# Moving the pieces of the next batch between the attention units of a fused audio tower

## The chip, the core and the metric

The kernel runs on one core of a Trainium2 chip. The time is the device time of one launch in microseconds (us); lower is better. TensorE is called PE, VectorE DVE, ScalarE ACT, GpSimd POOL; SP is the queue of SyncE, which here only issues DMAs.

## What is computed

The input is 8 rows of 120,000 samples, each cut into 1500 frames of 80. All arithmetic is float32 in the reference:

```python
h = layernorm(x_frames @ W.T + b) * gamma + beta          # 8 x 1500 x 256
h = gelu(h)                                               # exact, with erf
z = _layernorm(h)
Q, K, V = z @ Wq.T + bq, z @ Wk.T + bk, z @ Wv.T + bv      # 16 heads of 16
attn = softmax(Q K^T / 4)                                 # 1500 x 1500 per head
h = h + (attn V) @ Wo.T + bo
h = h + _L0_ffn_ref(_layernorm(h), ...)
```

The last line is computed in both kernels as `h + layernorm(_layernorm(h)) * ln_g + ln_b`: the routed attention inside `_L0_ffn_ref`, whose weights are drawn with a spread of 0.02, is in neither, and its weights are no inputs of them.

## The kernel before

**Units and rounds.** The attention of a batch is cut into 12 units (the text counts them from 0 to 11): 4 groups of 4 heads by 3 chunks of 500 queries. Unit u has group u // 3 and chunk u % 3, so units 9, 10 and 11 are the last group of a batch. A unit has 8 rounds (0 to 7). In each round PE multiplies six pairs of key tile and head into six PSUM banks (`scores`, L810, matmuls of float16), ACT takes the exponential of two banks at a time (lines 473, 476 and 481, in this order, are the three of a round), and PE multiplies the result with the values (`attend`, L834, float32): one tile of keys in an even round (4 matmuls side by side on the 128 columns of the array), two in an odd one. PE runs up to four scores matmuls ahead, those of the first two exponentials of the next round.

**Other work in between.** Everything else is cut into pieces, and the table `PLAN` says behind which round of which unit each is done. The pieces of batch b+1 are spread over the units of batch b, and so are the outputs of the batch before: 6 `tok` (tokenizer matmul of two tiles of frames, L755, then its layer norm on DVE with POOL's root between, L503 to L518), 6 `turn` (transposes, L764, and a copy on DVE, L542), 12 `qk` (projection in two halves, L771, each in a round of its own; behind the second half DVE writes it as two float16 tensors, L551 and L553, and SP stores them to a scratch in HBM), 12 `val` (values, L780 and L558), 3 `norm` and one `flag` (a bound on the scores' size, L787 and L793, that selects the softmax without a maximum), 12 `out` (output projection, L800, and the last layer norm, L612 to L625). Behind every fourth `qk`, POOL squares all four (L367).

**One bank for the pieces.** All pieces of a unit use one PSUM bank, 7 - n % 2 for unit n of the whole run. The other bank of the two collects the unit's attention. So PE waits in `beside` before each piece until DVE has freed the bank of the piece before, and before the first piece of a unit until DVE has taken the sums of the unit before out of that bank (`take_sums`, L595 and L596). DVE takes the pieces in the same order as PE issues them, and does between them: `invert` (four reciprocals, L603, behind rounds 1 to 4, and with the fourth the product L606), and three times in a batch, where the table `NORMS` says so, the layer norm of four tiles of the next batch (`norm_stats` and `norm_apply`, L526 to L535, with POOL's root between). These three stand behind the pieces and the reciprocal of their round.

**GELU.** ACT does the GELU of a whole batch at one place (`GELU`), between two loads of its table.

**SP's queue.** It is in program order too: the stores of `qk`; behind round 4 of a unit `store_attended`, which waits until DVE has finished L606 of the unit before; and `load_group`, which loads Q and K of the next four heads. The last scores that PE issues in round 7 of unit 2, 5, 8 and 11 are those of the next group and wait for that load (`s_ld`). For the groups 1 to 3 it is issued at the start of unit 1, 4 and 7. For the first group of the next batch:

```python
if u == NU - 1 and b + 1 < B:
    load_group((b + 1) * NG)
```

Of the kernel before, what the change touches and what calls it, by code (L numbers as in the profile page):

```python
# [5 lines left out]
def audio_tower(nc, x, tok_wT, tok_b, tok_g, tok_be, wqT, bq, wkT, bk, wvT, bv, woT, bo, ln_g, ln_b, out):  # L6
# [47 lines left out]
    place(2, 4, "turn", 0)
    place(2, 6, "turn", 1)
    place_qk(0, 3, 0, 2)
    place_qk(1, 3, 3, 4)
# [6 lines left out]
    place(5, 2, "val", 3)
    place(5, 3, "turn", 2)
    place(5, 4, "turn", 3)
    place(5, 6, "val", 4)
    place_qk(4, 6, 0, 2)
    place_qk(5, 6, 3, 4)
    place(6, 6, "val", 5)  # L70
    place_qk(6, 7, 0, 2)
    place_qk(7, 7, 3, 4)
    place(7, 6, "val", 6)
    place(8, 0, "val", 7)
    place(8, 1, "norm", 1)
    place(8, 2, "turn", 4)
    place(8, 3, "turn", 5)
    place_qk(8, 8, 4, 6)
    place_qk(9, 9, 0, 2)
    place_qk(10, 9, 3, 4)  # L80
    place(9, 6, "val", 8)
    place_qk(11, 10, 0, 2)
    place(10, 3, "val", 9)
    place(10, 4, "val", 10)
    place(10, 6, "val", 11)
    place(11, 1, "norm", 2)
    place(11, 5, "flag", 0)
# [50 lines left out]
    with ExitStack() as ctx:  # L138
# [86 lines left out]
        def at(sem_, count):  # L225
            return count + TOTAL.get(sem_, 0) if second[0] else count
# [6 lines left out]
        def _(sp):  # L233
# [38 lines left out]
            def store_out(b, c):  # L272
                k = b * NC + c
                sp.wait_ge(s_y, at(s_y, CT * (k + 1)))
                sp.dma_start(out_v[b, :, c * CT:(c + 1) * CT, :], Y[:, k % 2, :, :]).then_inc(s_yst[k % 2], 16)

            def run():
                load_x(1)
                for i in range(4 * NC):
                    store_halves(0, i)  # L280
                load_group(0)
                for n in range(B * NU):
                    b, u = n // NU, n % NU
# [211 lines left out]
        def _(dve):  # L495
# [11 lines left out]

            def tok_norm(b, i, bank):
                p, e = i % 2, hslot(b, 2 * i)
                dve.wait_ge(s_r1, at(s_r1, b * (NT // 2) + i + 1))  # L510
                for j in range(2):
                    ins = dve.scalar_tensor_tensor(out=Hs[:, e + j, :], in0=PS[0:T, bank, j * D:(j + 1) * D],  # L512
                                                   scalar=mv1[:, p, j, 0:1], in1=g_tok[:, :],
                                                   op0=ALU.subtract, op1=ALU.mult)
                ins.then_inc(s_free, 1)
                dve.drain()
                for j in range(2):
                    ins = dve.scalar_tensor_tensor(out=Hs[:, e + j, :], in0=Hs[:, e + j, :],  # L518
                                                   scalar=rs1[:, p, j:j + 1], in1=be_tok[:, :],
                                                   op0=ALU.mult, op1=ALU.add)  # L520
                ins.then_inc(s_h1, 1)
# [463 lines left out]
```

## Time and profile before

| | |
|---|---|
| median of 3 runs | 2575.2 us (2572.72 to 2577.77) |
| the profiled execution | 2566.03 us |
| its span, first to last instruction | 2564.3 us |
| PE busy | 2270.0 us, 89% |
| ACT busy | 2154.9 us, 84% |
| DVE busy | 1222.3 us, 48% |
| mean granted clock of TensorE | 0.952 of full |

Busy time of PE is that of pipelined matmuls whose ends are modelled, so 89% doesn't mean that it computed for 89% of the time. ACT's 2304 exponentials are the longest chain of one engine. A unit is measured here from the start of its first L473 to that of the next unit.

### The profile page before, as it was taken

To read this page: it belongs to the slowest core of one execution; us is meant where nothing else is said; L and a number is where in the kernel's file an instruction comes from. 1 tells how busy PE (TensorE), PEld (TensorE's weight loads), DVE (VectorE), ACT (ScalarE), POOL (GpSimd) and SP (SyncE) were. 2 spreads that over 40 slices of the span, in tenths; PEclk is the share of its full clock that TensorE was granted. 3 is DMA by queue.
4 is the path that set the end of the run, shared out by engine and by line. 5 is a ranking of instruction groups with operands and counts; after the bars stand their busy time and mean duration, and the time that the engine had idled before them with its cause. 6 is when DMAs were issued, how large, how long until landed. Compare 5 with 4: busy or idle time off the path is not lost.

```text
span 2564.3 us, 48095 instructions
## 1 busy us (share of the span) xinstructions
PE 2270.0 (89%) x19500; PEld 680.2 (27%) x19500; DVE 1222.3 (48%) x2362; ACT 2154.9 (84%) x2332; POOL 374.1 (15%) x495
## 2 busy tenths in 40 slices
PE   4589998999989998899988999899998999898892
PEld 1222222222322222222222222222222222222221
DVE  6444435544465444643456444654446444452224
ACT  0099997999969998899978999699997999799991
POOL 2211002211121111210122110211112111120002
PEclk7799999999989999999989999899998999999997
DMA  2402211222122122122112221212212212111101
GB/s 60 128 17 63 63 37 39 53 63 63 38 69 56 42 59 53 46 77 53 41 45 53 63 63 39 58 40 56 67 33 70 54 51 53 52 47 31 31 5 30
DMA packets 89956, 132.09 MB, mean 52 GB/s; under 512 B 12295, under 2 KB 69702, under 8 KB 89726
## 3 DMA queue, kind: packets, MB, share of 16 engines
q1 hardware_dynamic: 87190, 127.11, 19.1%
q8 instruction: 156, 2.56, 0.4%
q10 hardware_dynamic: 2536, 1.83, 0.3%
q14 instruction: 74, 0.61, 0.1%
HBM read 55.16 MB, written 61.44 MB: 45 GB/s over the span
## 4 chain that ended last, share of the span: by engine, by line
PE 40%; issue 34%; ACT 9%; POOL 9%; DVE 4%; POOLq 1%; DMA 1%; SPq 1%; DVEq 0%; ACTq 0%
PE PS L834 19%; PE PS L810 12%; PE PS L771 5%; ACT prob L476 4%; ACT prob L473 3%; POOL sq L367 3%; POOL Y L375 2%; PE PS L780 2%; POOL rs L377 2%; DVE HL L553 1%; POOL rs L348 1%; DVE HL L551 1%; POOLq L376 1%; DMA qk_halves_scratch<-HL 1%; ACT prob L481 1%
## 5 line engine op out<-in xcount | busy, mean ns | idle before, releaser
L834 PE MATMUL PS<-prob,Vst 125*32 125x500 f32 x9216 | 1149.8, 602 | 1.9 <-ACT prob L476 1.1
L481 ACT ACTIVATE prob<-PS 125x1000 f32<-125x1000 f32 x768 | 775.0, 1009 | 208.9 <-PE PS L810 208.3
L810 PE MATMUL PS<-QA,KA 64*125 64x500 f16 x4608 | 783.1, 413 | 105.2 <-DMA KA<-qk_halves_scratch 46.0
L473 ACT ACTIVATE prob<-PS 125x1000 f32<-125x1000 f32 x768 | 773.6, 1007 | 108.3 <-PE PS L810 108.2
L476 ACT ACTIVATE prob<-PS 125x1000 f32<-125x1000 f32 x768 | 782.8, 1019 | 0.0
L810 PEld LDWEIGHTS PS<-QA,KA 64*125 64x125 f16 x4608 | 258.7, 133 | 896.1 <-ACT prob L473 419.2
L603 DVE RECIPROCAL On<-Den 128x125 f32<-128x125 f32 x384 | 344.5, 918 | 10.2 <-issue 2.7
L834 PEld LDWEIGHTS PS<-prob,Vst 125*32 125x32 f32 x9216 | 221.9, 109 | 441.4 <-issue 272.9
L551 DVE TENSOR_SCALAR HL<-PS,b_qk 128x500 f16<-128x500 f32 x96 | 70.9, 738 | 397.9 <-PE PS L771 333.8
L367 POOL TENSOR_TENSOR sq<-HL 128x2000 bf16<-128x2000 f16 x24 | 84.5, 3522 | 1184.8 <-DVE HL L553 1184.8
L771 PE MATMUL PS<-zT,w_qk 128*32 128x500 f32 x1536 | 196.4, 593 | 1.2 <-DVE zT L542 1.2
L595 DVE LOAD_MASK_SELECT Den<-PS x96 | 1.3, 13 | 312.3 <-PE PS L834 312.3
L800 PE MATMUL PS<-w_o,oT 128*32 128x256 f32 (+1 forms) x1536 | 103.5, 391 | 37.6 <-DMA oT<-On 23.1
L780 PE MATMUL PS<-w_v,zT 128*32 128x256 f32 (+1 forms) x1536 | 104.7, 396 | 25.8 <-DVE Osb L596 25.8
L372 POOL TENSOR_SCALAR rs<-mv 125x1 f32<-125x1 f32 x96 | 26.7, 278 | 602.8 <-DVE mv L616 602.8
L558 DVE TENSOR_TENSOR Vst<-PS,b_v 125x256 f32<-125x256 f32 x96 | 40.2, 422 | 147.7 <-PE PS L780 147.7
L606 DVE TENSOR_TENSOR On<-On,Osb 128x500 f32<-128x500 f32 x96 | 101.0, 1052 | 7.9 <-issue 0.9
L755 PE MATMUL PS<-w_tok,X 81*32 81x256 f32 (+1 forms) x768 | 60.3, 445 | 31.7 <-DVE Hs L512 18.3
L625 DVE SCALAR_TENSOR_TENSOR Y<-Hs,rs,Y 125x256 f32<-125x256 f32 x96 | 79.7, 830 | 7.5 <-issue 0.4
L612 DVE TENSOR_TENSOR Hs<-Hs,PS 125x256 f32<-125x256 f32 x96 | 38.4, 400 | 93.8 <-PE PS L800 93.5
L771 PEld LDWEIGHTS PS<-zT,w_qk 128*32 128x32 f32 x1536 | 49.9, 112 | 115.9 <-issue 87.9
L542 DVE COPY zT<-PS 128x500 f32<-128x500 f32 x48 | 32.6, 679 | 94.4 <-PE PS L764 94.4
(78 smaller groups left out, 1068.4 us busy)
## 6 DMA issues: line engine op xcount, KB each, us to landing
qk_halves_scratch<-HL SPq DMA_DIRECT2D x384, 125.0 KB
QA<-qk_halves_scratch SPq DMA_DIRECT2D x64, 375.0 KB, 5.0
KA<-qk_halves_scratch SPq DMA_DIRECT2D x64, 375.0 KB, 7.2
oT<-On SPq DMA_DIRECT2D x384, 31.2 KB, 2.0
out<-Y SPq DMA_DIRECT2D x24, 500.0 KB
X<-in_x SPq DMA_DIRECT2D x8, 468.8 KB, 8.1
w_qk<-in_wqT ACTq DMA_DIRECT2D x2, 128.0 KB, 3.8
w_qk<-in_wkT ACTq DMA_DIRECT2D x2, 128.0 KB, 3.9
```

The source lines that it names most:

```text
L367: pool.tensor_tensor(sq[:, :, :], HL[:, :, 0, :], HL[:, :, 0, :], ALU.mult).then_inc(s_sq, 1)
L473: act.activation(prob[0:T, 6 * p:6 * p + 2, :], PS[0:T, 0:2, 0:QC], ACT.Exp, scale=scl)\
L476: act.activation(prob[0:T, 6 * p + 2:6 * p + 4, :], PS[0:T, 2:4, 0:QC], ACT.Exp, scale=scl)\
L481: act.activation(prob[0:T, 6 * p + 4:6 * p + 6, :], PS[0:T, 4:6, 0:QC], ACT.Exp, scale=scl)\
L551: dve.tensor_scalar(HL[:, i % 4, 0, :], PS[:, bank, 0:QC], bias, None, ALU.add)
L603: dve.reciprocal(On[:, part * T:(part + 1) * T], Den[:, part * T:(part + 1) * T])
L606: dve.tensor_tensor(On[:, :], On[:, :], Osb[:, :], ALU.mult).then_inc(s_on, 1)
L771: ins = pe.matmul(PS[lo:hi, bank, 0:QC], w_qk[:, c, w, m * 128 + lo:m * 128 + hi], zT[:, c, :], start=(c == 0), stop=(c == KC - 1))
L780: last = pe.matmul(PS[lo:hi, bank, 0:D], zT[:, c, t + lo:t + hi], w_v[:, c, :], start=(c == 0), stop=(c == KC - 1))
L800: last = pe.matmul(PS[lo:hi, bank, 0:D], oT[:, m, e * T + lo:e * T + hi], w_o[:, m, :], start=(m == 0), stop=(m == KC - 1))
L810: last = pe.matmul(PS[0:T, bank, 0:QC], KA[rows, G % 2, h // 2, t * T:(t + 1) * T], QA[rows, G % 2, h // 2, c * QC:(c + 1) * QC], start=Tr ...
L834: last = pe.matmul(PS[lo:lo + 2 * HD, 6 + n % 2, 0:QC], Vst[:, b % 2, t, g * HG + j, :], prob[0:T, (HG * t + j) % 12, :], start=(t == 0), ...
```

## The change

It moves pieces to other rounds, moves two of the three layer norms on DVE earlier and one later against the rounds, moves the GELU from round 7 of unit 1 to round 2 of unit 2, issues the load of the next batch's first group at the end of unit 10 in place of unit 11, stores the last outputs of a batch in unit 3 in place of unit 2, and in `tok_norm` on DVE puts the wait for POOL's root behind the first of two passes (a drain stands where it was).

```diff
-    for j, r in enumerate((0, 2, 3, 4)):
+    for j, r in enumerate((0, 2, 4, 6)):
         place(11, r, "out", j)
         place(0, r, "out", 4 + j)
-    for j in range(2):
-        place(11, 5 + j, "tok", j)
-        place(0, 5 + j, "tok", 2 + j)
-        place(1, 2 * j, "tok", 4 + j)
-    place(1, 4, "out", 8)
+    place(10, 4, "tok", 0)
+    place(11, 3, "tok", 1)
+    place(0, 3, "tok", 2)
     for j in range(3):
-        place(1, 6, "out", 9 + j)
+        place(1, 2 * j, "tok", 3 + j)
+        place(2, 1, "out", 9 + j)
+    place(1, 6, "out", 8)
...
-    NORMS = {(2, 0): 0, (4, 6): 1, (7, 6): 2}
-    GELU = (1, 7)
+    NORMS = {(2, 3): 0, (4, 4): 1, (6, 6): 2}
+    GELU = (2, 2)
...
-                    if u < 3 and b > 0:
-                        store_out(b - 1, u)
+                    if u in (0, 1, 3) and b > 0:
+                        store_out(b - 1, min(u, 2))
...
-                    if u == NU - 1 and b + 1 < B:
+                    if u == NU - 2 and b + 1 < B:
                         load_group((b + 1) * NG)
...
             def tok_norm(b, i, bank):
                 p, e = i % 2, hslot(b, 2 * i)
-                dve.wait_ge(s_r1, at(s_r1, b * (NT // 2) + i + 1))
+                dve.drain()
                 for j in range(2):
                     ins = dve.scalar_tensor_tensor(out=Hs[:, e + j, :], in0=PS[0:T, bank, j * D:(j + 1) * D],
                                                    scalar=mv1[:, p, j, 0:1], in1=g_tok[:, :],
                                                    op0=ALU.subtract, op1=ALU.mult)
                 ins.then_inc(s_free, 1)
                 dve.drain()
+                dve.wait_ge(s_r1, at(s_r1, b * (NT // 2) + i + 1))
```

The whole table, as pieces by unit and round (`/` parts rounds; qk3a and qk3b are the two halves of the fourth projection; N0, N1, N2 are DVE's layer norms):

| unit | before | after |
|---|---|---|
| 0 | 0 out, 2 out, 3 out, 4 out, 5 tok, 6 tok | 0 out, 2 out, 3 tok, 4 out, 6 out |
| 1 | 0 tok, 2 tok, 4 out, 6 three out, GELU ahead of 7 | 0 tok, 2 tok, 4 tok, 6 out |
| 2 | 0 N0, 4 turn, 6 turn | 1 three out, GELU ahead of 2, 3 N0, 6 turn |
| 3 | 0 qk0a, 2 qk0b, 3 qk1a, 4 qk1b, 6 val | 0 turn, 2 qk0a, 3 qk0b, 4 qk1a, 5 qk1b, 6 val |
| 4 | 0 qk2a, 2 qk2b, 3 qk3a, 4 qk3b, 6 val and N1 | 0 qk2a, 2 qk2b, 3 qk3a, 4 qk3b and N1, 5 val, 6 val |
| 5 | 0 val, 1 norm, 2 val, 3 turn, 4 turn, 6 val | 0 val, 1 norm, 2 turn, 3 turn, 4 qk4a, 6 qk4b |
| 6 | 0 qk4a, 2 qk4b, 3 qk5a, 4 qk5b, 6 val | 0 qk5a, 2 qk5b, 3 qk6a, 4 qk6b, 5 val, 6 val and N2 |
| 7 | 0 qk6a, 2 qk6b, 3 qk7a, 4 qk7b, 6 val and N2 | 0 qk7a, 2 qk7b, 3 val, 4 val, 6 turn |
| 8 | 0 val, 1 norm, 2 turn, 3 turn, 4 qk8a, 6 qk8b | 0 turn, 1 norm, 2 qk8a, 3 qk8b, 4 qk9a, 5 qk9b, 6 val |
| 9 | 0 qk9a, 2 qk9b, 3 qk10a, 4 qk10b, 6 val | 0 qk10a, 2 qk10b, 3 qk11a, 4 qk11b, 6 val |
| 10 | 0 qk11a, 2 qk11b, 3 val, 4 val, 6 val | 0 val, 1 norm, 2 val, 4 tok, 6 flag |
| 11 | 0 out, 1 norm, 2 out, 3 out, 4 out, 5 tok and flag, 6 tok | 0 out, 2 out, 3 tok, 4 out, 6 out |

Two places of it as the engines' own programs have them. The first is SP's queue at the end of the first batch, from the stores of the last projections on; oT<-On is the store of a unit's attention, QA and KA are the loads of a group. Before:

```order
148 L245 DMA qk_halves_scratch<-HL 8x16x500 [waits s_free]
149 L245 DMA qk_halves_scratch<-HL 8x16x500 x3
150 L269 DMA oT<-On 16x500 [waits s_on]
151 L269 DMA oT<-On 16x500 x3
152 L269 DMA oT<-On 16x500 [waits s_on]
153 L269 DMA oT<-On 16x500 x3
154 L258 DMA QA<-qk_halves_scratch 64x2x1500 [waits s_st,s_sc,s_ld]
155 L258 DMA QA<-qk_halves_scratch 64x2x1500
156 L258 DMA KA<-qk_halves_scratch 64x2x1500 x2
```

And in the change:

```order
148 L269 DMA oT<-On 16x500 [waits s_on]
149 L269 DMA oT<-On 16x500 x3
150 L269 DMA oT<-On 16x500 [waits s_on]
151 L269 DMA oT<-On 16x500 x3
152 L258 DMA QA<-qk_halves_scratch 64x2x1500 [waits s_st,s_sc,s_ld]
153 L258 DMA QA<-qk_halves_scratch 64x2x1500
154 L258 DMA KA<-qk_halves_scratch 64x2x1500 x2
155 L269 DMA oT<-On 16x500 [waits s_on]
156 L269 DMA oT<-On 16x500 x3
```

The load now stands ahead of the store of unit 10's attention (row 155) and behind that of unit 9's (row 150); before, it stood behind unit 10's (row 152).

The second place is DVE's queue in unit 4 of the first batch, from the second half of qk3 on; L526 to L535 are the layer norm N1, L595 and L596 take the sums of the unit, L558 takes a `val`. Before:

```order
192 L551 TENSOR_SCALAR HL<-PS,b_qk 128x500 [waits s_full,s_st]
193 L553 SCALAR_TENSOR_TENSOR HL<-PS,b_qk,HL 128x500
194 L603 RECIPROCAL On<-Den 128x125
195 L606 TENSOR_TENSOR On<-On,Osb 128x500
196 L558 TENSOR_TENSOR Vst<-PS,b_v 125x16x16 [waits s_full]
197 L526 BN_STATS st<-Hs 125x6 [waits s_ge]
198 L526 BN_STATS st<-Hs 125x6 x3
199 L529 BN_AGGR mv<-st 125x2 x4
200 L535 TENSOR_SCALAR z<-Hs,mv,rs 125x256 [waits s_r2]
201 L535 TENSOR_SCALAR z<-Hs,mv,rs 125x256 x3
202 L595 STREAM_SHUFFLE Den<-PS 128x500 [waits s_pv,s_on]
203 L596 COPY Osb<-PS 128x500
```

And in the change, where the lines of DVE from here on have a number that is higher by one:

```order
193 L552 TENSOR_SCALAR HL<-PS,b_qk 128x500 [waits s_full,s_st]
194 L554 SCALAR_TENSOR_TENSOR HL<-PS,b_qk,HL 128x500
195 L604 RECIPROCAL On<-Den 128x125
196 L607 TENSOR_TENSOR On<-On,Osb 128x500
197 L527 BN_STATS st<-Hs 125x6 [waits s_ge]
198 L527 BN_STATS st<-Hs 125x6 x3
199 L530 BN_AGGR mv<-st 125x2 x4
200 L536 TENSOR_SCALAR z<-Hs,mv,rs 125x256 [waits s_r2]
201 L536 TENSOR_SCALAR z<-Hs,mv,rs 125x256 x3
202 L559 TENSOR_TENSOR Vst<-PS,b_v 125x16x16 [waits s_full] x2
203 L596 STREAM_SHUFFLE Den<-PS 128x500 [waits s_pv,s_on]
204 L597 COPY Osb<-PS 128x500
```

The layer norm now stands ahead of the two takings of values (row 202); before, one of them stood ahead of it (row 196) and the next behind L596, in unit 5.

## Rows read from the trace of the kernel before

**Rows 1.** The page: busy time by engine, and two of its groups.

```profile
PE 2270.0 (89%) x19500; PEld 680.2 (27%) x19500; DVE 1222.3 (48%) x2362; ACT 2154.9 (84%) x2332; POOL 374.1 (15%) x495
...
L810 PE MATMUL PS<-QA,KA 64*125 64x500 f16 x4608 | 783.1, 413 | 105.2 <-DMA KA<-qk_halves_scratch 46.0
...
L558 DVE TENSOR_TENSOR Vst<-PS,b_v 125x256 f32<-125x256 f32 x96 | 40.2, 422 | 147.7 <-PE PS L780 147.7
```

**Rows 2.** Busy time by stretch: unit 3 of batch 7; all of batch 7; batch 2.

```profile
core 0: us, PE busy (x) PEld busy (x) DVE busy (x) ACT busy (x) POOL busy (x), PEclk, DMA share, GB/s
2311.25:2333.18 21.93, 19.48 (x148) 5.16 (x144) 5.29 (x8) 21.93 (x26) 0.00 (x0) 1.00 0.34 77
2238.81:2509.60 270.79, 243.53 (x1926) 67.22 (x1924) 90.93 (x156) 263.33 (x288) 19.22 (x36) 1.00 0.12 28
723.90:1027.49 303.59, 282.49 (x2439) 84.45 (x2437) 151.94 (x293) 269.48 (x291) 46.24 (x60) 0.96 0.21 53
```

**Rows 3.** The same: batch 3, units 0, 1, 3, 5, 8, 11.

```profile
1027.49:1056.96 29.47, 26.52 (x250) 8.32 (x248) 17.74 (x38) 22.16 (x25) 7.30 (x14) 0.91 0.09 27
1056.96:1086.10 29.14, 24.45 (x244) 7.67 (x240) 19.94 (x48) 27.34 (x30) 7.97 (x16) 1.00 0.27 65
1108.02:1130.85 22.83, 22.74 (x196) 6.41 (x192) 8.77 (x13) 21.99 (x25) 0.00 (x0) 1.00 0.17 50
1153.62:1179.84 26.22, 23.95 (x208) 7.60 (x204) 10.99 (x24) 22.05 (x26) 3.64 (x3) 0.93 0.05 10
1225.38:1251.54 26.16, 23.90 (x192) 7.15 (x188) 11.18 (x24) 22.02 (x25) 3.61 (x3) 0.93 0.05 10
1297.25:1331.12 33.87, 25.88 (x245) 8.59 (x237) 21.43 (x53) 22.17 (x25) 8.12 (x16) 0.88 0.24 56
```

**Rows 4.** Timeline, end of batch 3, SP and PE.

```profile
1318.55 2.40 SPq L269 DMA_DIRECT2D oT<-On  x4
1322.40 1.25 SPq L258 DMA_DIRECT2D KA<-qk_halves_scratch  x2
...
1321.67 0.37 PE L793 MATMUL PS<-ident,nm 128*1 128x128 f32 x1 [4.57 <-DVE Hs L512]
1330.41 1.09 PE L810 MATMUL PS<-QA,KA 64*125 64x500 f16 x4 [3.31 <-DMA KA<-qk_halves_scratch]
```

**Rows 5.** Timeline of PE in unit 4 of batch 3, rounds 4 and 5.

```profile
1144.06 0.85 PE L810 MATMUL PS<-QA,KA 64*125 64x500 f16 x6
1144.84 1.04 PE L834 MATMUL PS<-prob,Vst 125*32 125x500 f32 x8
...
1147.73 1.88 PE L834 MATMUL PS<-prob,Vst 125*32 125x500 f32 x16
```

**Rows 6.** Timeline, from there to unit 5: DVE, POOL and PE.

```profile
1148.49 3.52 POOL L367 TENSOR_TENSOR sq<-HL 128x2000 bf16<-128x2000 f16 x1 [51.34 <-DVE HL L553]
1149.33 3.21 DVE L606 TENSOR_TENSOR On<-On,Osb 128x500 f32<-128x500 f32 x1
1151.28 1.05 PE L780 MATMUL PS<-w_v,zT 128*32 128x256 f32 x16
1152.81 1.39 DVE L526 BATCH_NORM_STATS2 st<-Hs 125x6 f32<-125x256 f32 x4
1156.20 1.38 DVE L535 TENSOR_SCALAR z<-Hs,mv,rs 125x256 f32<-125x256 f32 x4 [1.55 <-POOL rs L354]
1158.83 1.73 PE L780 MATMUL PS<-w_v,zT 128*32 128x256 f32 x16 [1.86 <-DVE Osb L596]
```

**Rows 7.** Unit 5 of batch 1, by stretch as in rows 2.

```profile
547.84:572.48 24.64, 22.43 (x208) 7.26 (x204) 11.00 (x24) 22.06 (x26) 3.65 (x3) 1.00 0.05 12
```

**Rows 8.** Timeline of DVE in the prologue: the second and the third `tok`.

```profile
22.16 0.87 DVE L512 SCALAR_TENSOR_TENSOR Hs<-PS,mv,g_tok 125x256 f32<-125x256 f32 x2 [1.21 <-POOL rs L348]
23.12 0.88 DVE L518 SCALAR_TENSOR_TENSOR Hs<-Hs,rs,be_tok 125x256 f32<-125x256 f32 x2
...
26.20 0.88 DVE L512 SCALAR_TENSOR_TENSOR Hs<-PS,mv,g_tok 125x256 f32<-125x256 f32 x2 [1.20 <-POOL rs L348]
```

More of the change, by code:

```diff
@@ L42, in place_qk @@
         place(u, r1, "qk", i, True)
-    for j, r in enumerate((0, 2, 3, 4)):
+    for j, r in enumerate((0, 2, 4, 6)):
         place(11, r, "out", j)
         place(0, r, "out", 4 + j)
-    for j in range(2):
-        place(11, 5 + j, "tok", j)
-        place(0, 5 + j, "tok", 2 + j)
-        place(1, 2 * j, "tok", 4 + j)
-    place(1, 4, "out", 8)
-    for j in range(3):
-        place(1, 6, "out", 9 + j)
[L54 to L57, printed above, removed]
+    place(10, 4, "tok", 0)
+    place(11, 3, "tok", 1)
+    place(0, 3, "tok", 2)
+    for j in range(3):
+        place(1, 2 * j, "tok", 3 + j)
+        place(2, 1, "out", 9 + j)
+    place(1, 6, "out", 8)
+    place(2, 6, "turn", 0)
+    place(3, 0, "turn", 1)
+    place_qk(0, 3, 2, 3)
+    place_qk(1, 3, 4, 5)
     place(3, 6, "val", 0)
@@ L60, in audio_tower @@
     place_qk(3, 4, 3, 4)
-    place(4, 6, "val", 1)
-    place(5, 0, "val", 2)
+    place(4, 5, "val", 1)
+    place(4, 6, "val", 2)
+    place(5, 0, "val", 3)
     place(5, 1, "norm", 0)
[L64 to L69, printed above, removed]
-    place(6, 6, "val", 5)
[L71 to L74, printed above, removed]
-    place(8, 1, "norm", 1)
[L76 to L87, printed above, removed]
-    NORMS = {(2, 0): 0, (4, 6): 1, (7, 6): 2}
-    GELU = (1, 7)
+    place(5, 2, "turn", 2)
+    place(5, 3, "turn", 3)
+    place_qk(4, 5, 4, 6)
+    place_qk(5, 6, 0, 2)
+    place_qk(6, 6, 3, 4)
+    place(6, 5, "val", 4)
+    place(6, 6, "val", 5)
+    place_qk(7, 7, 0, 2)
+    place(7, 3, "val", 6)
+    place(7, 4, "val", 7)
+    place(7, 6, "turn", 4)
+    place(8, 0, "turn", 5)
+    place(8, 1, "norm", 1)
+    place_qk(8, 8, 2, 3)
+    place_qk(9, 8, 4, 5)
+    place(8, 6, "val", 8)
+    place_qk(10, 9, 0, 2)
+    place_qk(11, 9, 3, 4)
+    place(9, 6, "val", 9)
+    place(10, 0, "val", 10)
+    place(10, 1, "norm", 2)
+    place(10, 2, "val", 11)
+    place(10, 6, "flag", 0)
+    NORMS = {(2, 3): 0, (4, 4): 1, (6, 6): 2}
+    GELU = (2, 2)
     def batch_of(what, b, u):
@@ L94, in batch_of @@
         if what == "tok":
-            return b + 2 if u == NU - 1 else b + 1
+            return b + 2 if u >= NU - 2 else b + 1
         return b + 1
```

## The prediction, made before the changed kernel ran

> **What bounds the kernel now.** I read first the busy times of the page [rows 1]: ACT is busy 84%, PE 89%, DVE under half, so no engine is full, and the question is how far each unit is from what ACT alone needs. The busy times by stretch, cut at the starts of the units, tell that (in these rows stand the us, the busy us of each engine with its instructions, and the clock that was granted, 1.00 being 2.4 GHz). The floor is a unit of batch 7 with no piece in it: 21.93 us, and ACT is busy in all of it [rows 2]. A batch of twelve such units is 263 us. Batch 2 took 303.59, batch 7, which prepares no other batch, 270.79 [rows 2]. So each of the first seven batches loses some 40 us to the pieces, and the change can only win or lose among these.
>
> Where they are lost [rows 3]: a unit with pieces and nothing unusual takes 22.83 (units 3, 4, 6, 7, 9, 10 are all alike). Unit 0 takes 29.47, unit 1 29.14, units 5 and 8 26.2, unit 11 33.87. In unit 1 ACT is busy for 27.34 us, 5.4 more than elsewhere: that is the GELU, and it costs the same wherever it stands. The others are waits.
>
> Unit 11 and unit 0 are read in the timeline [rows 4]. PE waits 4.57 us ahead of the flag, since the `tok` before it holds the bank until DVE has POOL's root. Then it waits 3.31 us for the first group of the next batch: SP issued that load at 1322.40, behind the store that began at 1318.55 and had waited for DVE's L606, and it landed at 1330.4. Over all boundaries these waits are 46.0 us [rows 1]. Since the load lands 33 us after unit 11 began (1297.25), it ends the unit whatever the flag does. The granted clock of these two stretches is 0.88 and 0.91 of full [rows 3]: behind the waits TensorE runs for a while at 1.2 in place of 2.4 GHz.
>
> Units 5 and 8 [rows 6]: DVE begins the layer norm of round 6 of unit 4 at 1152.81 and ends its z at 1157.58, then takes the sums, and PE waits 1.86 us for those. If the clock stays at full the unit takes 24.64 [rows 7], at a granted 0.93 26.22 [rows 3].
>
> Why a normal unit costs 0.9 over the floor [rows 5, 6]: PE needs 0.85 for the six scores, 0.9 (a row of 1.04 that overlaps its neighbours) or 1.88 for the values, and 1.0 for a piece. Two rounds with one piece behind the even one are 5.5 us, ACT's two rounds also 5.5 (21.93 / 4). A second piece in the pair, behind the odd round, has no room: it costs 0.9 to 1.0. With two such pairs in one unit I count 1.8.
>
> **The change, part by part**, per batch, from the table of pieces.
>
> *Load in unit 10, flag in unit 10.* The load is issued behind the store of unit 9's attention. If DVE gives that free as late in unit 10 as it does in unit 11 now, 21.3 us in (1318.55 less 1297.25), and the issue and landing take the same 11.9 us as now, it lands 33 us after unit 10's start, 11 us into unit 11, and it is wanted in the last round, some 20 us in. All projections are stored by then. The flag has its `tok` two rounds behind it and doesn't wait. Unit 11 keeps one odd piece (0.9) and 0.3 for the round behind the `tok` (the bank comes free after 4.04 less 1.21 and 0.88, the period, wait and L518 of [rows 8], so 2.0; PE comes back after 0.85 and 0.9): 23.1 in place of 33.9, a gain of 10.8. Unit 0 loses its low clock, and one of two `tok` in neighbouring rounds: it keeps the odd piece (0.9), 0.3 behind the `tok`, and a wait at its start, since the last `out` now stands in round 6 of unit 11, and DVE finishes its layer norm before it takes the sums. That wait is between 0 and the 1.86 that a later DVE costs in [rows 6]; a layer norm of one tile is shorter than that of four, so I take 0.8. 23.9 in place of 29.5: a gain of 5.6.
>
> *Units 1 and 2.* GELU moves with its cover: the three `out` still run on PE while ACT is away. The first wait of unit 1 stays (now behind an `out`). I count nothing.
>
> *Unit 3* has pieces in rounds 3 and 5: +0.9. *Unit 6* too: +0.9. *Unit 8*: the same, but without the layer norm's wait: 26.2 to 23.9, a gain of 2.3. *Unit 10*: its pieces are light, a gain of 0.4.
>
> *Layer norm N1 in round 4 of unit 4* is what speaks against the change. DVE's queue holds it now ahead of the two takings of `val`. The round is the same in which POOL squares for 3.52 us and L606, normally 0.68, takes 3.21 until 1152.54 [rows 6]. The layer norm starts there as before (4.8 us from 1152.81 to 1157.58, no longer behind a `val` of 0.42 [rows 1]), z is done at 1157.2, the first `val` taken at 1157.6. PE wants the bank for the second `val` at 1151.28 [rows 6] plus the 1.0 of the new piece in round 5, at 1152.3. So it stands still for 5.3 us, and is 6.3 us later than before. ACT has two exponentials in hand, as always there, and loses all of it. A low clock comes on top: between 0 and 3 us; units 5 [rows 3, 7] show 1.6 behind a wait of 1.86, and behind a longer one I take 2. Unit 4: 22.8 to 31.1, a loss of 8.3. Unit 5 no longer has the wait: from 25.4 (the mean of the two above) to 22.8, a gain of 2.6.
>
> *N2 in round 6 of unit 6.* It does to unit 7 what N1 did to unit 5: a loss of 2.6 in place of those counted as gone in unit 8.
>
> Sum over a batch: -10.8 - 5.6 + 0.9 + 0.9 - 2.3 - 0.4 + 8.3 - 2.6 + 2.6 = -9.0, times seven -63 us.
>
> *`tok_norm`.* Ahead of L512 DVE waits 1.21 us for POOL, then L512 takes 0.87 and L518 0.88; the next L512 starts 4.04 later (22.16 to 26.20) [rows 8]. With L512 inside the wait the period is 0.9 shorter. In the prologue nothing else runs beside these six, and all waits for them: -5 us. The bounds are 0, if L512 held POOL off, and 0.9 x 6. The Trainium skill (SBUF — State Buffer, "Who interferes with whom") says that a VectorE instruction contends with GpSimd if both its inputs lie in SBUF; L512 reads one from PSUM, so the full gain would stand; no run here shows these two side by side yet. In the units it frees the bank sooner, which is counted above.
>
> *A cost that the trace can't show:* at a batch's start ACT waits for the flag's value and loads a register with the scale. Before, that lay in a wait of several us. Exposed it costs between 0 and about 1 us; I take 0.5, +3.5 in all.
>
> Batches 0 and 7 differ little (the three `out` without GELU cost in unit 2 what they cost in unit 1), and the end gains and loses about 1 us. Together -63 - 5 + 3.5 = -64.5. Against the profiled execution's 2566.0 this is 2501.5. The median of the runs is 9 us above that execution, so for the median I forecast 2511.
>
> **Rivals.**
> *No stall in unit 4.* If PE found the bank free in round 6 of unit 4, its 8.3 would shrink to the 1.0 of the odd piece: 7.3 x 7 = 51 us less, 2460. Against it stands DVE's order, in which nothing lets a `val` pass the layer norm. Chance 0.05.
> *A smaller gain at the boundary.* ACT may lose more behind GELU or at the start of units 0 and 1, where DVE is now late by its own sum; 2 to 5 us per batch, 14 to 35 in all: 2525 to 2545. The bounds of the 0.8 above are for it, the order of DVE is neither for nor against. Chance 0.14.
> *The load is still late* (the slower side). If SP were held so long that the load landed where it does now, 33 us into unit 11, units 11 and 0 would keep all but about 3 of their 16.4: 13.4 x 7 = 94 us more, 2605. A late landing eats the 64.5 us from 29 us into unit 11 on (20 and 64.5 / 7), 18 us later than I expect at the latest; nothing in SP's order does that. Chance 0.03.
> *The clock stays low after the stall in unit 4* (slower too). At 1.2 GHz PE needs twice its time and ACT waits for it; each us costs about half a us. To eat the 64.5 us it must hold 18 us per batch longer than I count. The longest low stretches here hold for part of two units at 0.88 and 0.91 [rows 3]. Chance 0.04: about 2590. The Trainium skill (TensorE: Matmul & The Clock Gate, Part 1) calls the low clock the default from which activity releases the engine, so by the page full work in round 7 and unit 5 would end it soon; the rows behind the 1.86 us wait agree, with a mean of 0.93 over the unit.
>
> **How the numbers follow.** The forecast itself (gains of 40 to 90 us) has 0.72; with the two rivals that also gain, faster is 0.72 + 0.14 + 0.05 = 0.91. The bound to "no change" is 0.2%, 5 us, which is about what the three runs scatter. No change has 0.02, slower the last two rivals' 0.07. Range: below, without 1.6 us of clock per stall and without the register -20 us, 2490; above, the smaller gain's 2545. That leaves out the stall-free case and the slower ones.
>
> **What would show it.** Unit 11 near 23 us and unit 0 near 24 at full clock; no wait for KA; unit 4 near 31 us with one PE wait of over 5 us at L781, ended by DVE's taking of the `val`; unit 5 near 23; unit 7 at 24 to 26; the period of the first `tok` at 3.1. I'd be wrong if unit 4 were near 24, or if unit 11 still waited for the load.

## The result, and the profile after

The changed kernel takes 2490.76 us (2489.94 to 2492.69, 4 runs) against 2575.28 (2572.72 to 2577.77); the ratio is 0.9673, interval 0.9656 to 0.969. Its profiled execution took 2490.91 us with a span of 2489.2. The profiled executions lie 75.1 us apart, the medians 84.5: the profiled one of the kernel before was quicker than all its plain runs, that of the changed kernel is in the middle of its own. Forecast were 2511 and a gain of 64.5 between the profiled ones.

The page of the changed kernel, the lines that answer to [rows 1] (PE's lines have a number higher by one now):

```profile
PE 2238.5 (90%) x19500; PEld 669.2 (27%) x19500; DVE 1231.5 (49%) x2362; ACT 2155.4 (87%) x2332; POOL 374.1 (15%) x495
...
L811 PE MATMUL PS<-QA,KA 64*125 64x500 f16 x4608 | 769.1, 406 | 85.0 <-ACT prob L476 45.6
...
L781 PE MATMUL PS<-w_v,zT 128*32 128x256 f32 (+1 forms) x1536 | 105.4, 398 | 38.1 <-DVE Vst L559 38.1
```

No engine does less or more; the busy time of PE fell by 32 us, with a mean granted clock of 0.970 against 0.952. The wait for KA is no longer the largest of the scores, and the values have a new one: 38.1 us in all, for DVE's L559.

By stretch, batch 3 as in [rows 3]: units 0, 1, 3, 4, 5, 7, 8 and 11, then all of batch 7 as in [rows 2]. The columns are those of [rows 2].

```profile
995.90:1020.27 24.37, 22.90 (x232) 7.20 (x224) 16.80 (x37) 22.05 (x25) 7.36 (x14) 1.00 0.09 27
1020.27:1043.38 23.11, 22.11 (x216) 6.80 (x208) 17.02 (x39) 21.94 (x25) 4.43 (x9) 1.00 0.40 95
1070.65:1094.43 23.78, 23.53 (x204) 6.63 (x196) 9.56 (x15) 22.19 (x25) 0.00 (x0) 1.00 0.20 59
1094.43:1124.61 30.18, 24.69 (x212) 7.21 (x208) 14.72 (x26) 22.05 (x25) 7.15 (x4) 0.93 0.40 103
1124.61:1148.79 24.18, 23.69 (x192) 6.96 (x192) 8.94 (x14) 21.95 (x26) 0.00 (x0) 0.95 0.03 6
1172.38:1196.98 24.60, 22.50 (x200) 6.73 (x196) 10.59 (x23) 22.04 (x25) 7.13 (x4) 1.00 0.39 90
1196.98:1220.97 23.99, 23.65 (x208) 6.75 (x200) 10.08 (x15) 22.19 (x25) 0.00 (x0) 1.00 0.12 33
1265.75:1289.17 23.42, 22.91 (x232) 7.30 (x224) 14.55 (x33) 22.14 (x25) 5.79 (x11) 1.00 0.32 73
2165.90:2434.50 268.60, 242.47 (x1924) 66.85 (x1916) 91.25 (x158) 263.34 (x289) 18.99 (x37) 1.00 0.12 30
```

Units 0 and 11 give back what they lost and their clock is full. Unit 4 (30.2) is the only long one left besides unit 2 with its GELU (27.3).

The boundary, to be read beside [rows 4]: SP's store of unit 9's attention, the load, the flag, and the first piece of the next batch's unit 0.

```profile
1263.93 2.40 SPq L269 DMA_DIRECT2D oT<-On  x4
1267.78 1.26 SPq L258 DMA_DIRECT2D KA<-qk_halves_scratch  x2
...
1263.62 0.27 PE L794 MATMUL PS<-ident,nm 128*1 128x128 f32 x1
...
1293.38 0.85 PE L801 MATMUL PS<-w_o,oT 128*32 128x256 f32 x12 [0.86 <-DVE Osb L597]
```

The load is out 2.0 us into unit 11 (1267.78 against 1265.75); before it went out 25 us into it. PE doesn't wait ahead of the flag, and nobody waits for the load. The last line is the new wait at the start of unit 0: forecast 0.8, measured 0.86.

Unit 4, beside [rows 6]: POOL, DVE, PE and ACT, and then a stretch behind the stall, for its clock.

```profile
1112.00 3.52 POOL L367 TENSOR_TENSOR sq<-HL 128x2000 bf16<-128x2000 f16 x1 [43.92 <-DVE HL L554]
1112.84 3.21 DVE L607 TENSOR_TENSOR On<-On,Osb 128x500 f32<-128x500 f32 x1
1112.93 1.05 PE L781 MATMUL PS<-w_v,zT 128*32 128x256 f32 x16
1119.37 1.38 DVE L536 TENSOR_SCALAR z<-Hs,mv,rs 125x256 f32<-125x256 f32 x4 [1.54 <-POOL rs L354]
1120.66 0.42 DVE L559 TENSOR_TENSOR Vst<-PS,b_v 125x256 f32<-125x256 f32 x1
1121.13 1.93 PE L781 MATMUL PS<-w_v,zT 128*32 128x256 f32 x16 [5.40 <-DVE Vst L559]
1123.71 1.00 ACT L481 ACTIVATE prob<-PS 125x1000 f32<-125x1000 f32 x1 [6.53 <-PE PS L811]
...
1121.00:1124.40 3.40, 3.27 (x22) 1.08 (x22) 0.50 (x2) 0.69 (x1) 2.18 (x1) 0.50 0.00 0
```

The value of round 5 is done on PE at 1114.0, but DVE takes it at 1120.66, behind L607 and the whole layer norm. PE's next piece waits 5.40 us. It then runs at a clock of 0.50, the lower of the two levels (1.2 GHz): its 16 matmuls take 1.93 us instead of 1.05, and ACT has stood still for 6.53.

The prologue, beside [rows 8]:

```profile
20.01 0.88 DVE L512 SCALAR_TENSOR_TENSOR Hs<-PS,mv,g_tok 125x256 f32<-125x256 f32 x2
21.13 0.88 DVE L519 SCALAR_TENSOR_TENSOR Hs<-Hs,rs,be_tok 125x256 f32<-125x256 f32 x2 [0.24 <-POOL rs L348]
...
23.10 0.88 DVE L512 SCALAR_TENSOR_TENSOR Hs<-PS,mv,g_tok 125x256 f32<-125x256 f32 x2
```

The wait of 1.21 us is down to 0.24 and the period from 4.04 to 3.09.

### The profile page after: what moved, and what is told of

Read it like the earlier page. It is cut to its first block, busy times and chain, and to the rows that moved or that the text cites. A ratio compares the mean times of both kernels' runs of the same rounds, so it can differ in the third digit from the quotient of the medians.

```text
span 2489.2 us, 48115 instructions
## 1 busy us (share of the span) xinstructions
PE 2238.5 (90%) x19500; PEld 669.2 (27%) x19500; DVE 1231.5 (49%) x2362; ACT 2155.4 (87%) x2332; POOL 374.1 (15%) x495
## 3 DMA queue, kind: packets, MB, share of 16 engines
q10 hardware_dynamic: 2536, 1.83, 0.3%
## 4 chain that ended last, share of the span: by engine, by line
issue 47%; PE 27%; ACT 10%; POOL 8%; DVE 3%; POOLq 1%; DMA 1%; SPq 1%; DVEq 0%; ACTq 0%
PE PS L835 12%; PE PS L811 8%; PE PS L772 5%; ACT prob L476 4%; ACT prob L473 4%; POOL sq L367 2%; POOL Y L375 2%; POOL rs L377 2%; ACT prob L481 2%; POOLq L376 1%; PE PS L781 1%; PE PS L756 1%; DVE z L536 1%; SPq L245 1%; POOL rs L354 1%
## 5 line engine op out<-in xcount | busy, mean ns | idle before, releaser
L835 PE MATMUL PS<-prob,Vst 125*32 125x500 f32 x9216 | 1132.0, 594 | 0.2 <-ACT prob L476 0.2
L811 PE MATMUL PS<-QA,KA 64*125 64x500 f16 x4608 | 769.1, 406 | 85.0 <-ACT prob L476 45.6
L367 POOL TENSOR_TENSOR sq<-HL 128x2000 bf16<-128x2000 f16 x24 | 84.5, 3520 | 741.7 <-DVE HL L554 741.7
L781 PE MATMUL PS<-w_v,zT 128*32 128x256 f32 (+1 forms) x1536 | 105.4, 398 | 38.1 <-DVE Vst L559 38.1
L801 PE MATMUL PS<-w_o,oT 128*32 128x256 f32 (+1 forms) x1536 | 101.5, 385 | 41.8 <-DMA oT<-On 23.1
L596 DVE LOAD_MASK_SELECT Den<-PS x96 | 1.4, 14 | 275.0 <-PE PS L835 275.0
L607 DVE TENSOR_TENSOR On<-On,Osb 128x500 f32<-128x500 f32 x96 | 110.8, 1154 | 7.5 <-issue 0.4
L559 DVE TENSOR_TENSOR Vst<-PS,b_v 125x256 f32<-125x256 f32 x96 | 40.3, 423 | 92.6 <-PE PS L781 92.6
L781 PEld LDWEIGHTS PS<-w_v,zT 128*32 128x32 f32 (+1 forms) x1536 | 47.1, 112 | 116.7 <-DVE Vst L559 44.4
L801 PEld LDWEIGHTS PS<-w_o,oT 128*32 128x32 f32 (+1 forms) x1536 | 45.8, 110 | 118.0 <-issue 30.6
L626 DVE SCALAR_TENSOR_TENSOR Y<-Hs,rs,Y 125x256 f32<-125x256 f32 x96 | 72.9, 760 | 7.5 <-issue 0.4
```

The lines of the kernel that those rows point to most:

```text
L367: pool.tensor_tensor(sq[:, :, :], HL[:, :, 0, :], HL[:, :, 0, :], ALU.mult).then_inc(s_sq, 1)
L607: dve.tensor_tensor(On[:, :], On[:, :], Osb[:, :], ALU.mult).then_inc(s_on, 1)
L626: dve.scalar_tensor_tensor(out=y, in0=h, scalar=rs3[:, n % 2:n % 2 + 1], in1=y, op0=ALU.mult, op1=ALU.add).then_inc(s_y, 1)
L781: last = pe.matmul(PS[lo:hi, bank, 0:D], zT[:, c, t + lo:t + hi], w_v[:, c, :], start=(c == 0), stop=(c == KC - 1))
L801: last = pe.matmul(PS[lo:hi, bank, 0:D], oT[:, m, e * T + lo:e * T + hi], w_o[:, m, :], start=(m == 0), stop=(m == KC - 1))
L811: last = pe.matmul(PS[0:T, bank, 0:QC], KA[rows, G % 2, h // 2, t * T:(t + 1) * T], QA[rows, G % 2, h // 2, c * QC:(c + 1) * QC], start=Tr ...
```

## The experiments

The theory in all of them: a unit costs ACT's 21.9 us plus what PE is late for the pieces, and PE is late for three reasons: two pieces in a pair of rounds (0.9), a bank or the sums that DVE frees late, and a group of heads that isn't loaded. A low clock can follow the last two. Eleven kernels were run, four from the changed kernel, four from the kernel before, and three that go on. Each ratio is to the kernel before on the same chip.

### Undoing N1's place

```diff
-    NORMS = {(2, 3): 0, (4, 4): 1, (6, 6): 2}
+    NORMS = {(2, 3): 0, (4, 6): 1, (6, 6): 2}
```

> The changed kernel with the layer norm N1 moved from round 4 of unit 4 back to round 6, behind both takings of values; the pieces stay. Theory (the stall of 5.4 us in unit 4 is PE waiting for the bank that a value holds behind N1 in DVE's queue): the wait moves to the first piece of unit 5 and shrinks to 1.7 to 1.9 us as in unit 7, unit 4 takes 23.8 us instead of 30.2, unit 5 24.6 to 26.2 instead of 23.7; together 4 to 5.5 us less in each of seven batches, so 2452 to 2463 us. Rival (the loss in unit 4 comes from the value piece in the odd round 5 and from POOL's squares holding DVE, not from N1's place): unit 4 stays near 30 and the time at 2491.

Measured 2460.91 us, ratio 0.9567 (0.9546 to 0.9587). Units 4 and 5 of batch 3:

```profile
1082.83:1107.21 24.38, 23.58 (x216) 6.83 (x208) 12.45 (x17) 22.05 (x25) 3.52 (x1) 1.00 0.49 126
1107.21:1131.76 24.55, 22.32 (x192) 6.73 (x188) 11.12 (x24) 21.94 (x26) 3.63 (x3) 1.00 0.03 8
```

So the change's own place of N1 cost some 28 us (28.4 between the profiled executions, 27 by the ratios). The rival is out: with the value still in round 5 and POOL's squares where they were, unit 4 falls from 30.2 to 24.4.

### Both layer norms where no piece waits

```diff
-    NORMS = {(2, 3): 0, (4, 4): 1, (6, 6): 2}
+    NORMS = {(2, 3): 0, (4, 0): 1, (6, 0): 2}
```

> The changed kernel with N1 in round 0 of unit 4 and N2 in round 0 of unit 6, where the first piece is the first half of a projection, which DVE doesn't take. Theory (a layer norm of 4.8 us on DVE costs nothing where no piece waits for DVE within two rounds): unit 4 23.8 us, unit 7 22.8, no PE wait of over 1 us in units 4, 6 and 7; 8.3 us less in each of seven batches, so 2433 us, 2428 to 2442. Rival (DVE has no room anyway; the late reciprocals of unit 4 and 6 delay the taking of the projection in round 2, and the wait only moves there): no more gain than with N1 behind the values, 2455 or above.

Measured 2431.49 us, ratio 0.9453 (0.9434 to 0.9473). Units 4, 5 and 7 of batch 3:

```profile
1070.19:1094.57 24.38, 23.57 (x216) 6.83 (x208) 14.72 (x26) 22.05 (x26) 7.17 (x4) 1.00 0.50 125
1094.57:1117.19 22.62, 22.11 (x192) 6.84 (x188) 8.94 (x14) 21.94 (x26) 0.00 (x0) 1.00 0.04 8
1140.79:1163.59 22.80, 22.49 (x200) 6.82 (x196) 8.45 (x13) 21.94 (x26) 3.52 (x1) 1.00 0.41 98
```

Unit 7 is now as short as a normal unit, and unit 5 shorter. The same work on DVE costs 57 to 59 us in one place (by the ratios, and between the medians) and next to nothing four and six rounds earlier. Unit 4 keeps 0.6 more than the 23.8 of unit 3, which has pieces in as many rounds: DVE takes the value of round 5 only behind L607, which takes 3.21 us beside POOL's squares, and PE waits 0.71 us for it. N1 has no part in that, for with N1 in round 6 the wait was the same 0.71. No run moved the squares.

### The load late again

```diff
-                    if u == NU - 2 and b + 1 < B:
+                    if u == NU - 1 and b + 1 < B:
```

> The changed kernel with the load of the next batch's first group issued at the end of unit 11 again. Theory (the load's landing ended unit 11, whatever the flag did): SP issues it behind the store of unit 10's attention, it lands some 33 us into unit 11, unit 11 takes 33 us instead of 23.2, unit 0 some 2 more for a low clock; 11 to 13 us in each of seven batches, 2568 to 2582 us, all of what the change gained. Rival (the flag with its wait of 4.6 us was a part of the loss, and with it moved the load is wanted late enough): 5 to 7 us per batch, 2526 to 2540.

Measured 2569.29 us (10 runs), ratio 0.9991 (0.9981 to 1.0): the whole gain is gone. Unit 11 of batch 3, and PE and SP in it:

```profile
1298.81:1332.88 34.07, 22.68 (x224) 7.27 (x216) 16.91 (x36) 22.24 (x26) 7.41 (x14) 0.90 0.25 60
...
1324.14 1.26 SPq L258 DMA_DIRECT2D KA<-qk_halves_scratch  x2
...
1332.16 1.09 PE L811 MATMUL PS<-QA,KA 64*125 64x500 f16 x4 [10.88 <-DMA KA<-qk_halves_scratch]
```

The wait is 10.88 us, not the 3.31 of [rows 4], with the landing at the same distance of 33 us from the start of the unit. The waits that the pieces of unit 11 made had hidden the difference before. The kernel before shows this in its own trace: at the last boundary, from batch 6 to 7, there is no `tok` and no wait ahead of the flag, and unit 11 still takes 33.9 us, with this wait at its end:

```profile
2238.10 1.09 PE L810 MATMUL PS<-QA,KA 64*125 64x500 f16 x4 [11.89 <-DMA KA<-qk_halves_scratch]
```

### The load early, alone, in the kernel before

```diff
-                    if u == NU - 1 and b + 1 < B:
+                    if u == NU - 2 and b + 1 < B:
```

> The kernel before with one edit: the load of the next batch's first group is issued at the end of unit 10. Theory (the load ended unit 11, and behind it the flag's wait is the next bound): the wait for KA goes, the wait of 4.6 us ahead of the flag stays, with a low clock behind it; unit 11 takes 28 to 30 us instead of 34, unit 0 26 to 28 instead of 29.4; 5 to 8 us in each of seven batches, 2515 to 2536 us. Rival 1 (the load alone was the loss): unit 11 near 24, 2460 to 2475. Rival 2 (without the flag's move nothing is gained): 2565 or more.

Measured 2521.9 us, ratio 0.9808 (0.979 to 0.9826). Unit 11 of batch 3, and what it waits for:

```profile
1281.19:1311.92 30.73, 26.03 (x253) 8.62 (x245) 19.68 (x49) 22.11 (x26) 7.26 (x15) 0.89 0.26 60
...
1305.63 0.37 PE L793 MATMUL PS<-ident,nm 128*1 128x128 f32 x1 [4.58 <-DVE Hs L512]
```

Unit 11 gives back 3 of its 34 us and unit 0 one (28.3), which leaves both longer than the 28 to 30 and 26 to 28 that were expected. The flag's wait is untouched and is the next bound. The total is in the expected range for another reason: at the last boundary, where no `tok` and so no flag's wait stands, unit 11 gives back 10.5 us (23.4 instead of 33.9), and this profiled execution lost the clock in units 5 and 8 less often than that of the kernel before, which is 6 us of the 46 between them. So by the medians' ratio 49 us go with this one line; the rest of unit 11 and unit 0 needs the flag and the tokenizer pieces moved away.

### N1 in round 4, alone, in the kernel before

```diff
-    NORMS = {(2, 0): 0, (4, 6): 1, (7, 6): 2}
+    NORMS = {(2, 0): 0, (4, 4): 1, (7, 6): 2}
```

> The kernel before with one edit: N1 in round 4 of unit 4 instead of round 6, with the pieces as before, so that round 5 has none. Theory (N1's place costs only if a piece is taken behind it whose bank PE wants within the 4.8 us): no stall in unit 4, which stays at 22.8; the only value of the unit is now taken behind N1, and so are the sums, so the wait of 1.9 us in unit 5 stays: no change, within 3 us of before. Rival (a layer norm in that round costs 6 us in itself, since POOL's squares hold DVE there): unit 4 near 29, 40 us slower.

Measured 2574.13 us (10 runs), ratio 1.0001 (0.9989 to 1.0014). Units 4 and 5 of batch 3, and PE at the start of unit 5:

```profile
1136.34:1159.12 22.78, 22.69 (x196) 6.41 (x192) 11.97 (x16) 21.97 (x26) 3.52 (x1) 1.00 0.47 116
1159.12:1185.35 26.23, 24.02 (x208) 7.63 (x204) 11.01 (x24) 22.04 (x26) 3.64 (x3) 0.93 0.05 10
...
1163.13 1.04 PE L834 MATMUL PS<-prob,Vst 125*32 125x500 f32 x8 [1.64 <-DVE Vst L558]
1164.34 1.85 PE L780 MATMUL PS<-w_v,zT 128*32 128x256 f32 x16 [0.17 <-DVE Osb L596]
```

The same place of N1 costs nothing here and some 28 us in the changed kernel. What makes the stall is the pair: a layer norm in round 4 and a piece in round 5 that DVE takes behind it, with another in round 6. The wait in unit 5 is as long as before but in two parts: 1.64 us ahead of the first values of the unit, which go into the bank that the last piece of unit 4 had, and 0.17 for the sums.

### Both layer norms in round 0, in the kernel before

```diff
-    NORMS = {(2, 0): 0, (4, 6): 1, (7, 6): 2}
+    NORMS = {(2, 0): 0, (4, 0): 1, (7, 0): 2}
```

> The kernel before with one edit: N1 in round 0 of unit 4 and N2 in round 0 of unit 7, where only the first half of a projection stands; all pieces as before. Theory (units 5 and 8 lose to the layer norm ahead of take_sums, 1.9 us and 1.6 more where the clock falls): both take 22.6 to 22.9 us; 5 to 6.5 us less in each of seven batches, 2525 to 2540 us. Rival (the layer norms' cost moves with them into units 4 and 7): 2565 or more.

Measured 2529.76 us (2528.67 to 2531.4), ratio 0.9843 (0.9823 to 0.9862). Units 5 and 8 take 22.7 us in every batch. Two numbers of the table give half as much as the whole change did.

### The tokenizer's layer norm, undone and alone

Undone in the changed kernel:

```diff
-                dve.drain()
+                dve.wait_ge(s_r1, at(s_r1, b * (NT // 2) + i + 1))
...
                 dve.drain()
-                dve.wait_ge(s_r1, at(s_r1, b * (NT // 2) + i + 1))
```

> The changed kernel with the wait for POOL's root ahead of both passes of the tokenizer's layer norm again. Theory (it pays in the prologue, 0.9 us for each of six, and where a piece stands in the round behind a tokenizer piece, so in units 11 and 0): 5.5 us in the prologue and 0.9 us at each of 14 places, 2509 us, 2504 to 2514. Rival (only the prologue is bound by DVE): 2496.

Measured 2515.19 us, ratio 0.978 (0.976 to 0.98), 24 us above the changed kernel (28 by the ratios) and just outside what was expected. In the profile 6.2 are in the prologue (the first exponential at 123.48 instead of 117.29) and 1.1 in each unit 0 and 11 (25.5 and 24.5 us) but the last unit 11, which has no `tok`, some 14 for the thirteen. Two units, 7 and 11, took 26.4 and 26.3 us once each, at a clock of 0.94, which is most of the rest.

The same order alone in the kernel before:

> The kernel before with the new order inside the tokenizer's layer norm alone (the wait for POOL's root behind the first pass). Theory: 5.5 us in the prologue, 0.9 us at each of the two places in units 0 and 1 where the round behind a tokenizer piece has another, nothing in unit 11, which the load ends: 18 us less, 2548 to 2558 us. Rival (only the prologue): 2565 to 2570.

Measured 2549.89 us, ratio 0.9916 (0.9897 to 0.9936), about 22 us by the ratio. The profiled execution was the slowest of the four and is 11.5 us below that of the kernel before; its units 5 and 8 lost the clock more often, which took back 4. The first exponential stands at 118.0 us instead of 122.8, and unit 0 takes 27.4 to 28.3 us instead of 29.5, unit 1 mostly 28.2. Unit 11 still takes 34, which the load sets.

### One odd piece fewer

From here on the edits go on from the kernel with both layer norms in round 0.

```diff
     for j, r in enumerate((0, 2, 4, 6)):
         place(11, r, "out", j)
-        place(0, r, "out", 4 + j)
+    for r, j in ((0, 4), (2, 5), (6, 6)):
+        place(0, r, "out", j)
...
-    place(0, 3, "tok", 2)
+    place(0, 4, "tok", 2)
+    place(1, 0, "out", 7)
     for j in range(3):
-        place(1, 2 * j, "tok", 3 + j)
+        place(1, 2 * j + 2, "tok", 3 + j)
+    place(2, 0, "out", 8)
+    for j in range(3):
         place(2, 1, "out", 9 + j)
-    place(1, 6, "out", 8)
```

> The kernel with both layer norms in round 0, and one piece fewer behind an odd round: the tokenizer piece of unit 0 goes from round 3 to 4, the three pieces behind it one place later each, the last of them to round 0 of unit 2. Theory (a second piece in a pair of rounds has no room on PE and costs 0.9, a tokenizer piece with the wait of 0.4 behind it 1.3): unit 0 23.1 us instead of 24.4, and since unit 2 has room in round 0, nothing is added: 7 x 1.0 to 1.3, 2422 to 2425 us. Rival (the pieces' sum counts, not where they stand): 2431.

Measured 2428.13 us, ratio 0.9439 (0.9422 to 0.9456), 3.5 us better than the one before it by the ratio, where 7 to 9 were expected; the intervals overlap, so that the size is read from the profile, 3.0. Unit 0 falls from 24.4 to 23.1 as forecast, but unit 2 rises from 27.2 to 27.4 or 28.0, and batch 7, where no GELU covers the outputs, from 268.6 to 270.5. The place that I had taken for empty, round 0 of unit 2, isn't free: DVE now does the last two passes of its output between the takings of the three of round 1, and PE waits 1.52 us ahead of the third (L804, for DVE's L616) where it had waited 0.55. In three batches the clock then falls, to 0.94 over the unit.

### A tokenizer piece last

```diff
-    for j, r in enumerate((0, 2, 4, 6)):
+    for j, r in enumerate((0, 2, 3, 4)):
         place(11, r, "out", j)
+    for j, r in enumerate((0, 2, 4)):
         place(0, r, "out", 4 + j)
+        place(1, r + 2, "tok", 3 + j)
     place(10, 4, "tok", 0)
-    place(11, 3, "tok", 1)
-    place(0, 3, "tok", 2)
+    place(11, 6, "tok", 1)
+    place(0, 6, "tok", 2)
+    place(1, 0, "out", 7)
+    place(2, 0, "out", 8)
     for j in range(3):
-        place(1, 2 * j, "tok", 3 + j)
         place(2, 1, "out", 9 + j)
-    place(1, 6, "out", 8)
```

> As the one with one odd piece fewer, and with a tokenizer piece instead of an output piece in round 6 of units 11, 0 and 1. Theory (the wait of 0.86 us ahead of the first piece of units 0 and 1 is DVE finishing the output's layer norm with POOL's root before it takes the sums; a tokenizer piece ends 0.8 us sooner on DVE, and no piece stands in the next round to wait for its bank): units 0 and 1 0.8 us less each, unit 11 0.4 less: 2.0 x 7 = 14 us below the other, 2407 to 2412. Rival (the tokenizer piece is as long on DVE, 3.3 us to 4.0): no difference.

Measured 2423.55 us, ratio 0.9423 (0.9406 to 0.944), 4 us better by the ratio where 14 were forecast, and outside the expected 2407 to 2412. Unit 11 gained its 0.5, but units 0 and 1 gained nothing: my theory of the wait at their start was not complete. DVE and PE at the start of unit 1:

```profile
992.81 0.88 DVE L521 SCALAR_TENSOR_TENSOR Hs<-Hs,rs,be_tok 125x256 f32<-125x256 f32 x2 [0.24 <-POOL rs L350]
993.61 0.48 DVE L625 SCALAR_TENSOR_TENSOR Hs<-Hs,mv,g_ln 125x256 f32<-125x256 f32 x1
...
995.91 0.85 PE L803 MATMUL PS<-w_o,oT 128*32 128x256 f32 x12 [0.81 <-DVE Osb L599]
```

Behind the tokenizer's last pass stands L625, a pass of the output of round 4. The loop on DVE keeps the last two passes of an output until the next piece has been taken, to hide POOL's root, and so puts them ahead of the sums.

### Those passes sooner

```diff
                         finish = (pb, i) if what == "out" else None
+                    if finish is not None and not pieces(b, u, r):
+                        finish_out(*finish)
+                        finish = None
```

> As the kernel with a tokenizer piece last, and with one edit on DVE: the last two passes of an output's layer norm no longer wait for the next piece, but are done in the next round if that has no piece. Theory (what still makes the first piece of units 0 and 1 wait 0.8 us is DVE doing those passes of the output before, 1.0 us, behind the tokenizer piece of round 6): the wait falls to 0 to 0.2, units 0 and 1 take 22.3 us instead of 23.1; 7 x 1.6 = 11 us less, 2410 to 2416. Rival (the tokenizer piece itself is too long): no difference.

Measured 2413.24 us, ratio 0.9386 (0.9367 to 0.9405), 9.5 us better by the ratio where 11 were forecast. Units 0 and 1 of batch 3:

```profile
963.40:985.87 22.47, 22.12 (x216) 6.78 (x208) 14.38 (x34) 22.02 (x25) 5.68 (x12) 1.00 0.12 34
985.87:1007.98 22.11, 21.98 (x216) 6.79 (x208) 15.63 (x38) 21.95 (x26) 4.30 (x10) 1.00 0.40 96
```

Unit 1 is within 0.2 us of the floor. This is the best kernel of the study, 6.1% below the kernel before and some 3% below the change.

## Why the prediction was right

The sum was made by unit, and can be checked by unit. The median lies inside the stated range of 2490 to 2545, but by 0.8 us only, and 20 us below the forecast of 2511. So the mechanism was right in its parts, while that the range held was luck. Batch 3:

| unit | before | forecast | measured |
|---|---|---|---|
| 0 | 29.5 | 23.9 | 24.4 |
| 1 and 2 | 51.1 | as before | 50.4 |
| 3 | 22.8 | 23.7 | 23.8 |
| 4 | 22.8 | 31.1 | 30.2 |
| 5 | 26.2 | 22.8 | 24.2 |
| 6 | 22.8 | 23.7 | 23.6 |
| 7 | 22.8 | 25.4 | 24.6 |
| 8 | 26.2 | 23.9 | 24.0 |
| 10 | 22.8 | 22.4 | 22.1 |
| 11 | 33.9 | 23.1 | 23.4 |

Batch 3 is one of seven, and over the seven the errors partly cancel. Unit 0 gave 31.4 us where 39.2 were forecast (in batch 0 it has no outputs, and gave 1.4), unit 5 gave 11.8 for 18.2. Units 1 and 2 gave 6.8 for nothing, unit 4 lost 52.3 for 58.1, unit 7 13.1 for 18.2. Why units 1 and 2 gained is open, since no run moved the GELU or the pieces there alone.

*The load and the flag.* Right in place and size: units 11 and 0 gave back 15.6 us of the 16.4 forecast. That the landing ends the unit whatever the flag does is shown from both sides, by the load put back (82 us lost by the ratios, 78.5 between the profiled executions) and by the load moved alone (49 gained by the ratio, and then the flag's wait of 4.58 is the bound).

*Odd rounds.* Units 3 and 6 came out within 0.1 us.

*N1 in unit 4.* The stall was forecast at 5.3 us and measured at 5.40. The low clock behind it cost less in unit 4 and ran on into unit 5, which has a clock of 0.95 and 1.4 us more than forecast; the two together were 0.5 us off. Over the seven batches unit 5 took 22.7 to 24.4. Undone it gives some 28 us.

*N2 in unit 7.* The wait came as forecast, 1.70 us, and the clock stayed full in all seven batches: 0.8 less each. The forecast had taken the mean of both cases here and in unit 5; for unit 8 it took 26.2, the low-clock case, though the same mean would have made its gain 1.5 instead of 2.3. Measured over seven batches it was 1.9.

*`tok_norm`.* -5 forecast, 5.5 measured in the prologue (kernels with the same prologue differ there by up to 1.4). L512 ran beside POOL's root and wasn't held up: 0.88 for its two instructions, against 0.87 before. The new order also mattered in the units, where it is worth some 14 more.

*The sum.* Between the first exponentials of batch 0 and batch 7 lie 2116.0 us before and 2048.7 after, a gain of 67.4 for the forecast 63. The prologue gave 5.5 and the part from batch 7 on 2.2, forecast 5 and about nothing. The register load at a batch's start, for which 3.5 us were set aside, was a price that no row showed, and it costs nothing to be seen: the first exponential of batch 4 starts at 1289.17, 0.90 after the last of batch 3, the same step as between any two there. These make the 75.1 of the profiled executions instead of 64.5.

*Where the 20 us are.* 10.6 are the sum: 4.4 in the batches, 3.5 the register load, 0.5 the prologue and 2.2 the end. The other 9.4 are the last step, in which 9 us were added for the way from the profiled execution to the median. In the kernel before that distance was real, in the changed kernel it is nil (2490.91 and 2490.76). The kernel before ran from 2566 to 2579 us over all its comparisons. Its units 5 and 8 take 24.6 or 26.2 us, by whether the clock falls behind a wait of 1.9 us [rows 3, 7], and there are fourteen such places. In the profiled execution of 2566.03 the clock fell in nine of them. In that of the kernel with N1 in round 4, which takes 2578.08, it fell in all fourteen, and units 5 and 8 make 7.9 of the 12 us between the two. So a part of the scatter was of the same cause as the loss, and an offset taken from the old kernel isn't carried to the new one. The plain runs have no trace, but their mean clocks point the same way, without proving it: the two slowest of the kernel before (2578.3 and 2578.8) had 0.947, and none under 2570 had less than 0.950.

The lower bound of the range, 2490, is 20 to 21 us below the forecast. Its two terms give 15 if the 1.6 us of clock are counted once per batch (2496, which the measured time would have missed) and 20 if units 4 and 7 are both meant (1.6 and 0.8). The prediction doesn't say which.

The rivals: none came. The stall in unit 4 was there, the load was in time, and the clock was full again by unit 6. The smaller gain had a DVE late at the start of units 0 and 1; it was late by 0.86 us, no more than was counted.

## What to carry to other kernels

Where one engine takes pieces in a fixed order and another waits for a shared buffer, a long step has a price only if a piece stands behind it that is wanted before it ends: 4.8 us of DVE cost 0 in the rounds ahead of an untaken piece, 1.9 at the end of a unit, and 6 to 7 between two pieces in neighbouring rounds. A late transfer and other waits ahead of it cover one another: the wait for it in the trace (3.3 us) is no measure of what moving it gives (some 4 us in an ordinary batch alone, nearly 12 when the other waits are gone too); ask when it lands. Steps held back to hide a latency should be let go as soon as there is an empty slot, not at the next piece.

## What was not expected of the hardware

A wait of PE of under 2 us can be enough for the clock to fall, and it isn't so each time. Behind the wait of 1.86 us in unit 5, the profiled execution of the kernel before ran at 1.00 over the unit in four batches and at 0.93 in three, and behind 1.83 us in unit 8 at 0.93 in six of seven. That of the kernel with N1 in round 4 ran at 0.93 in all of both. In the changed kernel none of the seven units 7 lost its clock behind 1.70 us or more. A fallen clock makes 1.6 us each time. Behind the thirteen waits of 0.86 to 0.94 us at the starts of units 0 and 1 in the changed kernel, the clock stayed at 1.00.

L607 on DVE (two inputs in SBUF) takes 3.21 us instead of 0.68 while POOL's L367 runs, in all fourteen places where the two meet, before and after; the reciprocal in the same stretch, with one input, keeps its 0.93. L512, whose other input lies in PSUM, ran beside POOL's root and kept its 0.88.
